# Second layer's channel mixture with each sample on its own half of the array's rows, both halves of a tile in one block

## The reference

```python
# second condition step: agg_w is 32 x 64 x 64, one matrix per sample
agg_w = jnp.einsum('bk,koi->boi', att, weight[..., 0])
out = jnp.einsum('boi,bih->boh', agg_w, x) + (att @ bias_k)[:, :, None]
# second dense step
base_out = jnp.einsum('bsd,od->bso', x, W_base) + b_base
weights = sparsemax(jnp.einsum('bsd,ed->bse', x, W_router) + b_router)
h = jnp.einsum('bsd,edr->bser', x, lora_A)
return base_out + jnp.einsum('bser,bse,ero->bso', h, weights, lora_B)
```

## Time and profile before

| | |
|---|---|
| median of 3 runs | 516.77 us (515.95 to 518.27) |
| the profiled execution | 515.9 us, of it 514.2 us span |
| instructions | 8712 |
| TensorE matmul busy | 506.9 us (99%) |
| TensorE weight load busy | 478.9 us (93%) |
| VectorE, ScalarE, GpSimd busy | 68%, 26%, 28% |
| granted TensorE clock | 1.0 of full |

### The profile page before, as it was taken

One profiled execution on the slowest core, in us unless ns is written; L12 is line 12 of the kernel. 1 busy time (PEld: TensorE's weight loads), 2 busy tenths in 40 slices (PEclk: granted clock), 3 DMA queues, 4 the chain that ended last, 5 costly groups with the idle time before them and its releaser, 6 DMA issues.

```text
span 514.2 us, 8712 instructions
## 1 busy us (share of the span) xinstructions
PE 506.9 (99%) x3231; PEld 478.9 (93%) x3231; DVE 351.3 (68%) x765; ACT 131.5 (26%) x272; POOL 142.2 (28%) x122
## 2 busy tenths in 40 slices
PE   8999999999999999999999999999999999999997
PEld 8999999999999999999999889999999999999986
DVE  3856988747576675766797576685848668584852
ACT  4732343312223122331352221211212121111200
POOL 1000010003443141433113372441706244170620
PEclk9999999999999999999999999999999999999999
DMA  8734304428376664647798942333315233430312
GB/s 339 290 129 135 124 1 146 153 87 269 111 240 229 215 223 164 202 156 256 256 421 288 407 164 87 132 97 127 136 63 171 75 120 106 134 135 18 107 41 82
DMA packets 40806, 85.31 MB, mean 166 GB/s; under 512 B 3739, under 2 KB 24731, under 8 KB 40764
## 3 DMA queue, kind: packets, MB, share of 16 engines
q1 hardware_dynamic: 31308, 60.89, 34.8%
q10 hardware_dynamic: 9456, 23.86, 12.4%
HBM read 59.30 MB, written 25.44 MB: 165 GB/s over the span
## 4 chain that ended last, share of the span: by engine, by line
PE 84%; DMA 8%; POOL 3%; DVE 2%; issue 1%; ACT 1%; SPq 0%; DVEq 0%; ACTq 0%; POOLq 0%
PE b_x L1188 6%; PE b_x L1190 6%; PE b_x L1191 6%; PE b_m L1139 5%; PE b_p L1173 4%; PE b_p L1172 4%; PE b_p L1174 4%; PE b_y L1188 4%; PE b_y L1191 4%; DMA x_scratch<-xs 4%; PE b_y L1190 4%; PE b_m L1149 2%; DMA xs<-x_scratch 2%; PE b_z L1190 2%; PE b_z L1191 2%; PE b_z L1188 2%
## 5 line engine op out<-in xcount | busy, mean ns | idle before, releaser
L529 ACT CAST a_hi<-mixed 128x512 fp32r<-128x512 f32 x63 | 38.1, 619 | 168.9 <-DVE mixed L821 91.5
L478 POOL TENSOR_TENSOR xs<-xs,mixw_sb 128x464 f32<-128x464 f32 (+1 forms) x32 | 44.5, 1399 | 124.5 <-DMA xs<-x_scratch 121.5
L833 DVE TENSOR_TENSOR s_lo<-mixed,s_hi 128x512 fp32r<-128x512 f32 x56 | 64.6, 1175 | 17.4 <-ACT s_hi L541 15.5
L1173 PE MATMUL b_p<-wp_lo,a_hi 128*128 128x232 f32 (+1 forms) x224 | 61.7, 275 | 0.0
L1172 PE MATMUL b_p<-wp_hi,a_hi 128*128 128x232 f32 (+1 forms) x224 | 61.4, 274 | 0.0
L1174 PE MATMUL b_p<-wp_hi,a_lo 128*128 128x232 f32 (+1 forms) x224 | 61.3, 274 | 0.0
L914 DVE TENSOR_TENSOR xs<-b_x,xs 128x464 f32<-128x464 f32 (+1 forms) x58 | 36.0, 621 | 30.4 <-PE b_x L1191 24.1
L541 ACT CAST s_hi<-mixed 128x512 fp32r<-128x512 f32 x56 | 34.8, 621 | 75.6 <-POOL mixed L451 36.0
L826 DVE TENSOR_TENSOR a_lo<-mixed,a_hi 128x512 fp32r<-128x512 f32 x64 | 44.7, 721 | 11.8 <-ACT a_hi L529 10.6
L451 POOL TENSOR_TENSOR mixed<-mixed 128x512 f32<-128x512 f32 x13 | 16.8, 1293 | 118.7 <-DVE a_lo L826 118.7
L1188 PE MATMUL b_x<-wb_hi,s_hi 128*128 128x464 f32 (+1 forms) x112 | 43.0, 384 | 1.1 <-DVE xs L914 1.0
(11 more groups left out here) (240 smaller groups left out, 1202.2 us busy)
## 6 DMA issues: line engine op xcount, KB each, us to landing
blk<-x_scratch SPq DMA_DIRECT2D x16, 512.0 KB, 3.9
blk<-in_xblk SPq DMA_DIRECT2D x15, 516.0 KB, 3.8
xs<-in_x SPq DMA_DIRECT2D x16, 296.0 KB, 4.5
x_scratch<-xs SPq DMA_DIRECT2D x16, 296.0 KB, 3.6
xs<-x_scratch SPq DMA_DIRECT2D x16, 280.0 KB, 3.1
out_dram<-xs SPq DMA_DIRECT2D x16, 280.0 KB, 2.4
w_raw<-in_wcat SPq DMA_DIRECT2D x8, 546.0 KB, 9.5
praw<-in_wcat ACTq DMA_DIRECT2D x8, 464.0 KB, 4.6
```

Source lines behind the costliest of these rows:

```text
L478: pool.tensor_tensor(xs[s][:, a:b], xs[s][:, a:b], bbase[:, a:b], ALU.add).then_inc(x_biased[q], 1)
L529: act.copy(a_hi[:, op, :, :], mixed[:, op, :, :]).then_inc(ahi_done[op], 1)
L833: dve.tensor_tensor(s_lo[:, i, :, :], mixed[:, S_AT[i], :, :], hi(s_hi[:, i, :, :]), ALU.subtract).then_inc(slo_done[i], 1)
L1173: pe.matmul(dst, x_hi, wp_lo[:, k, 0:PLAIN[l]], start=False, stop=False)
```

## The change

The second layer's mixture of one tile becomes one block of 16 matmuls. Each takes one sample: its 64 partitions of `blk` as stationary operand (64 rows x 128 positions) and its 64x64 quarter of `agg` as moving operand, so it is 64 columns wide. Sample 0 lies on partitions 0 to 63 and writes the tile's first bank, sample 1 on partitions 64 to 127 and writes the second, and the two take turns. Nothing is issued where half 0 stood; the block stands where half 1 stood. A bank now holds all 8 chunks of one sample, as in the first layer, so `sum_mix` has the first layer's form in both and every `split_a` waits for both sums of its tile. VectorE's sum of the odd tile's first bank moves behind `take(b_x, 1, ...)` from pass 7 on.

```diff
 def split_a(op, g):            # ScalarE
     T = 2 * g + op // 2
-    if layer(g) == 0:
-        act.wait_ge(sum_done, 2 * T + 2)
-    else:
-        act.wait_ge(sum_done, 2 * T + 1 + op % 2)
+    act.wait_ge(sum_done, 2 * T + 2)
...
 # VectorE, sum_mix
-                if T < TILES:
-                    row = ctx_row[:, s:s + 1, CH * n:CH * n + CH].to_broadcast([P, POS, CH])
...
-                else:
-                    row = ctx_row[:, s:s + 1, :].to_broadcast([P, HK, P])
-                    dve.tensor_tensor(mixed[:, 2 * s + n, :, :], src[:, :].rearrange("p (a c) -> p a c", c=P), row,
-                                      ALU.add).then_inc(sum_done, 1)
+                row = ctx_row[:, s:s + 1, CH * n:CH * n + CH].to_broadcast([P, NCH, CH])
+                dst = mixed[:, 2 * s:2 * s + 2, :, CH * n:CH * n + CH].rearrange("p q a c -> p (q a) c")
+                dve.tensor_tensor(dst, src[:, :].rearrange("p (a c) -> p a c", c=CH), row, ALU.add).then_inc(sum_done, 1)
...
-                if g < LAST and g != PAIRS:
+                if g + 1 < PAIRS:
                     sum_mix(2 * g + 3, 0)
...
                 take(b_x, 1, g, took_u2)
-                if g == PAIRS:
+                if PAIRS - 1 <= g < LAST:
                     sum_mix(2 * g + 3, 0)
...
 # TensorE
+                for k in range(NCH):
+                    for n in range(2):
+                        rows_ = slice(CH * n, CH * n + CH)
+                        ins = pe.matmul(banks[n][:, k * CH:(k + 1) * CH], blk[s][rows_, k * P:(k + 1) * P],
+                                        agg[rows_, s, rows_], start=True, stop=True)
+                        if k == NCH - 1:
+                            ins.then_inc(mix_done, 1)
+
+            def mixture(T, n, banks):
                 if T < TILES:
-                    conv_half(T, n, dst_bank)
-                else:
-                    mix_half(T, n, dst_bank)
+                    conv_half(T, n, banks[n])
+                elif n == 1:
+                    mix_samples(T, banks)
...
-                    mixture(t1 + 2, 1, b_y)
+                    mixture(t1 + 2, 1, (b_m, b_y))
...
-                    mixture(t2 + 2, 1, b_z)
+                    mixture(t2 + 2, 1, (b_m, b_z))
```

More of the change, by code:

```diff
@@ L814, in sum_mix @@
                 src = mix_bank(T, n)
-                if T < TILES:
-                    row = ctx_row[:, s:s + 1, CH * n:CH * n + CH].to_broadcast([P, POS, CH])
-                    dst = mixed[:, 2 * s:2 * s + 2, :, CH * n:CH * n + CH].rearrange("p q a c -> p (q a) c")
-                    dve.tensor_tensor(dst, src[:, :].rearrange("p (a c) -> p a c", c=CH), row, ALU.add).then_inc(sum_done, 1)
-                else:
-                    row = ctx_row[:, s:s + 1, :].to_broadcast([P, HK, P])
-                    dve.tensor_tensor(mixed[:, 2 * s + n, :, :], src[:, :].rearrange("p (a c) -> p a c", c=P), row,
-                                      ALU.add).then_inc(sum_done, 1)
+                row = ctx_row[:, s:s + 1, CH * n:CH * n + CH].to_broadcast([P, NCH, CH])
+                dst = mixed[:, 2 * s:2 * s + 2, :, CH * n:CH * n + CH].rearrange("p q a c -> p (q a) c")
+                dve.tensor_tensor(dst, src[:, :].rearrange("p (a c) -> p a c", c=CH), row, ALU.add).then_inc(sum_done, 1)
             def split_a(op, g):
@@ L1141, in conv_half, with mix_samples @@
                 ins.then_inc(mix_done, 1)
-            def mix_half(T, b, dst_bank):
+            def mix_samples(T, banks):
                 s = T % 2
@@ L1396, in _ @@
                     pe.wait_ge(sum_done, 2 * (t2 + 1))
-                    mixture(t1 + 2, 0, b_m)
+                    mixture(t1 + 2, 0, (b_m, b_y))
                 turn_u(t1)
@@ L1422, in _ @@
                 if g < LAST:
-                    mixture(t2 + 2, 0, b_m)
+                    mixture(t2 + 2, 0, (b_m, b_z))
                 if g == FULL:
```

## The result

The changed kernel takes 529.72 us (median of 4 runs, 528.65 to 530.91) against 517.52 us for the kernel before in the same comparison (4 runs, 515.95 to 520.35): ratio 1.024, 95% interval 1.021 to 1.027. That is 12.2 us slower; 6.0 were forecast. The profiled execution is the slowest of its four, 530.91 us with a span of 529.2, at a granted clock of 0.997 of full, while the one shown of before was the fastest of its own. So between the two profiles there are 15.0 us (the last matmul starts at 525.39 against 510.38 us), and between the medians 12.2.

A forecast was written before the change was run, and what follows sets the result against it. TensorE was taken to bound the kernel except at the turn. 12 tiles x 0.33 us of form switching (4.0) plus the turn (2.0) gave +6.0 on the median 516.8, so 522.8 us, range 516 to 550.

The forecast's parts named there:

- What bounds the kernel: TensorE, busy 99% of the span, sets the time, except at the turn between the layers.
- The pace of a step: In the mixture block, a record with 128 weight columns costs 0.11 us however narrow its moving operand is.
- Overlap of the row halves: In the block, two records on different row halves pass in the time of one: 16 steps, 1.78 us, no change.
- rival (a): No overlap of the row halves in the block: 2.11 us more a tile, +31.9, 549 us; chance 0.20.
- (b): Half overlap of the row halves in the block: 1.22 us more a tile, +18, 535 us; chance 0.13.
- (c): Block faster, its load halved or hidden and streaming setting the pace: steps of 0.056 us, -5.8, 511 us; chance 0.08.
- In and out of the 64-row form: Switching TensorE into and out of 64-row matmuls costs 0.33 us per tile, 0 to 0.5; 4.0 us for 12 tiles.
- What the move does to VectorE: The later sums on VectorE cost nothing in a steady pass, as P5 behind P4 needs the result next.
- The turn: Between the layers, A11's later cast delays B21's load by 3.4 us and the store chain by 2.0, 0 to 3.4.
- Rival (d): No switch cost for 64 rows and enough DMA work queued at the turn: 0 to +2, 517.8 us; chance 0.12.

The follow-up runs named there:

- e5: e1 with its block reordered, all 8 matmuls of sample 0 and then all 8 of sample 1: 561.6 us against 516.91.
- e6: e1 with each matmul of the block 32 moving columns wide instead of 64: 527.8 us against 516.91, a pass 30.61 us.
- e7: e1 with 64 weight columns in each matmul of the block instead of 128: 510.18 us against 516.91, a pass 28.96 us.
- e1: The changed kernel with VectorE doing split_ut(2g) ahead of the even tile's first sum from pass 7 on: 521.47 us against 516.13, ratio 1.012.
- e3: The changed kernel with full-height matmuls in the late block and split_ut(2g) ahead of the even tile's first sum: 515.87 us, ratio 1.001.
- e9: e2 with its full-height matmuls reordered so that the two banks take turns: 523.74 us against 516.76, a pass 31.13 us.
- e2: The changed kernel with its late block made of 8 full-height matmuls, one bank after the other, sums in the old form: 519.98 us, ratio 1.007.
- e4: e1 with the load of slot B21 issued ahead of the cast of A11 in pass 7: 521.0 us, ratio 1.009.
- e11: The kernel before, with ScalarE's pass 8 loads held until the turn's stores had landed: 516.53 us, ratio 0.999.

## Why the prediction was right or wrong

**What bounds the kernel: right.** Every microsecond that the steady passes gained or lost is a gap or a step on TensorE, and in e5 its clock.

**The pace of a step: right**, by e6 and e7: 0.11 us with 128 weight columns, with 64 moving columns as with 32.

**Overlap of the row halves: right.** Pairs start up to 0.01 us apart, and e5 shows the price without it, 1.4 us a block (the bound for rival (a) was 1.78). Rivals (a), (b) and (c) fall with the block's 1.93 us.

**In and out of the 64-row form: right in size**, 0.30 and 0.34 us a tile against 0.33, though the price had come from one 8-row matmul. The idle time ahead of the block that was forecast (0.28) is there in the loads (0.31), but it isn't the price. For an even tile of e1 against before the matmuls lose 0.09 us where the form is entered, 0.05 in the first step, which takes 0.16 instead of 0.11, and 0.09 at the end, where the transposes start 0.20 instead of 0.11 us behind the last record (for an odd tile 0.20 instead of 0.03). It was charged for 12 tiles. In e1 against e3 the medians are 5.6 us apart, where 12 tiles give 3.6 and 16 give 4.8, which their scatter can't decide; the profile of after closes with all 16, as shown below. Rival (d) falls too.

**What the move does to VectorE: wrong, and this is the step that failed.** It said that "who needs the result next is P5, behind P4 of 12 matmuls: nothing." It asked who needs the sum's *result*, and not who needs what is queued *behind the sum* on VectorE. That is `ut_lo` of the even tile, and the wait of `turn_u(2g+1)` on `utlo_done` stands directly behind the block on TensorE. So a term put at nothing is 1.17 us in each steady pass (after against e1), in all eight even tiles 9.4 us, of which the 9.1 us behind the blocks in the line for `b_u` are the idle part. What made it that long is that the sum now waits for the whole block, because both banks are completed by its last two matmuls (e9 costs 1.06 us a pass, e2, with one bank after the other, 0.40). It could be found blind. The prediction's own paragraph on the turn has "two sums of 0.68 and a split_ut between them" behind the block, but asks only when ScalarE's cast comes, and it checked `turn_u`'s margin to the gate (2.6 us), not that to `ut_lo`. The size was there too: a sum of about 0.6, `ut_lo`'s 0.28 and the latencies behind the block's end.

**The turn: not borne out.** 2.0 us were forecast. The cast of A11 came where it was put (256.65 against "near 257.0"), and the load 2.6 us later rather than 3.4. But e4, which takes that delay away, gained only 0.5 us, inside the intervals; e3 loses nothing; and in the profile of after the first quarter was ready on GpSimd 0.2 us later than before, and TensorE's wait in pass 8 was for VectorE's queue. By medians once the wait is out (e1) 0.5 to 1.7 us are left, which may be nothing. The mechanism that was argued, an empty stretch of the DMA queue, is not shown by any run.

**How it adds up.** Between the two profiles, passes 9 to 14 have 10.4 us more: six waits of 1.17 and twelve tiles of 0.30 are 10.6. Passes 7 and 8 have 5.2 more: two waits, of about 1.3 and 1.2, four tiles of 0.30, and the half clock's 1.56 behind the first of the new gaps are 5.3. The other waits of pass 8 are as long as before together (1.6 and 0.3 us, against 1.0, 0.8 and 0.1). That leaves about nothing for the turn in this execution. So the missed wait is 9.5 us, the form 4.8 and the half clock 1.6, 15.9 in all, and the rest of the program is 0.6 shorter: the 15.0 us to within 0.3. The medians are 12.2 apart, and by medians e1 gives back 12.2 - 5.3 = 6.9 and not 9.4. In e1 the waits of pass 8 can take the place of what the block's wait had covered; that is argued, not shown. That the forecast had half of the measured loss is in part luck: its turn of 2.0 stands in the sum where the runs show about nothing.

**A faster version.** None beat the kernel before. e3 and e11 equal it.

## What to carry to other kernels

When a block of work moves, list for each engine that consumes it not only who needs the result but every instruction queued behind the consumer, and the waits of the other engines on those; here one small split behind a sum cost more than all that the change did to TensorE itself. Then work out the new distance from the block's end to that user, and don't trust the cover of before: `ut_lo` had mostly been done 1.1 us or more ahead of its user, and came 1.2 us late once the sum ahead of it waited for the block. If outputs of a block are to be used in turn, complete them in turn: filling two banks in alternation makes the first consumer wait for the whole block.

Packing two 64-row matmuls side by side gained nothing here, as each still had 128 weight columns and a step stayed at 0.11 us. It needed alternate issue to break even (1.93 us a block against 3.32), and cost 0.3 us a block for going in and out of the form.

## What the runs showed of the hardware that I had not expected

The granted clock fell to 0.50 behind a gap of 1.25 us that followed a block of half-height matmuls, in pass 7 of the changed kernel, but not behind the seven later gaps of 1.12 us. In e5 it fell to 0.50 at 375.7 us, inside a block of half-height matmuls issued one by one, with no gap in TensorE's row. In e5, where sample 0's matmuls are all ahead of sample 1's in program order, records of the two halves are mixed at the change, and one of sample 1 starts before one of sample 0:

```profile
325.60 0.32 PE L1145 MATMUL b_y<-agg,blk 64*128 64x64 f32 x1
325.70 0.27 PE L1145 MATMUL b_m<-agg,blk 64*128 64x64 f32 x1
```

So, as the profiler has it, a matmul on the second half of the rows started ahead of its place in the program; all 16 blocks of e5 show this.
